# Eight extra two-byte matmuls behind each step's sum, and two-byte chunk tables, in a four-layer graph network

## The reference, cut to what matters

```python
def gcn_conv(x, src, dst, W, b, n_nodes):          # layer 0, twice
    h = x @ W
    msg = h[src] * (dinv[src] * dinv[dst])[:, None]
    return jax.ops.segment_sum(msg, dst, num_segments=n_nodes) + b

for _ in range(3):                                 # layer 1
    p = softmax(einsum('ecd,ecd->ec', z, u[trg]))  # z = xc[src]
    u = _l2norm(segment_sum(z * p[:, :, None], trg) + xc)

msg_sum = segment_sum(feature[src], dst)           # layer 2
h = relu((msg_sum / deg_safe[:, None]) @ W + b)

h = gelu(concatenate([H[src], edge_attr]) @ W1 + b1)   # layer 3
x = layernorm(H + segment_sum(h @ W2 + b2, dst)) * gamma + beta
```

## Time and profile before

| What | Value |
|---|---|
| Median of 3 runs | 6748.66 us (6747.69 to 6758.79) |
| Profiled execution, its span from first to last instruction | 7795.8 us |
| TensorE busy / VectorE / ScalarE / GpSimd in the span | 52% / 42% / 14% / 58% |
| Mean granted TensorE clock | 0.665 |
| CONV1, CONV2, MEAN in the span | 1146, 1138, 1142 us |
| CAPS1, CAPS2, CAPS3, EDGE in the span | 1407, 509, 510, 1347 us |

### The profile page before, as it was taken

How to read it: one execution, slowest core, us unless ns; L and a number is a source line. 1 busy time by engine, 2 the same in 40 slices (tenths; PEclk the granted TensorE clock), 3 DMA queues, 4 the chain that set the end, 5 groups by cost and what they waited for, 6 DMA issues and landing times.

```text
span 7795.8 us, 105357 instructions
## 1 busy us (share of the span) xinstructions
PE 4038.3 (52%) x24944; PEld 3239.4 (42%) x24945; DVE 3241.9 (42%) x8240; ACT 1099.4 (14%) x2520; POOL 4491.4 (58%) x4619
## 2 busy tenths in 40 slices
PE   0333334333333455555558868823333347777776
PEld 0323323333233345544557767713333334444443
DVE  4222213222124555555578888842221243333335
ACT  0000000000001222222233343310000021111112
POOL 4666665666664555555535535546666635555553
PEclk9656656556566676667789989955665565555555
DMA  3111112111111333333347757711111111111111
GB/s 98 44 45 45 45 46 54 44 46 45 45 45 29 118 118 119 118 118 119 120 151 224 225 176 228 223 47 44 45 45 45 45 41 38 38 39 38 39 38 39
DMA packets 354854, 637.41 MB, mean 82 GB/s; under 512 B 85485, under 2 KB 120442, under 8 KB 354170
## 3 DMA queue, kind: packets, MB, share of 16 engines
q0 software_dynamic: 127936, 263.97, 13.5%
q10 hardware_dynamic: 105408, 191.94, 7.9%
q1 hardware_dynamic: 121466, 181.04, 6.8%
HBM read 500.81 MB, written 135.79 MB: 82 GB/s over the span
## 4 chain that ended last, share of the span: by engine, by line
another core or an unknown queue 35%; PE 24%; issue 16%; DVE 12%; DVEq 5%; DMA 4%; ACT 3%; ACTq 1%; SPq 0%; POOL 0%; POOLq 0%
PE ps_sum L606 15%; PE ps_u L661 4%; PE ps_u L639 4%; DMA hots<-hot_rows 3%; DVE zu L1190 2%; DVE onehot L1000 2%; DVEq L241 2%; DVE acc L1014 1%; DVEq L1014 1%; DVE logit L1199 1%; ACT hots L808 1%; PE ps_a L656 1%; DVE prob_n L1174 1%; ACT onehot L818 1%
## 5 line engine op out<-in xcount | busy, mean ns | idle before, releaser
L525 POOL DMA_INDIRECT ring<-table,rows_idx x3920 | 3874.4, 988 | 2436.8 <-issue 1126.9
L606 PE MATMUL ps_sum<-ring,onehot 128*128 x5856 | 1202.3, 380 | 2328.5 <-DVE onehot L1000 1047.7
L606 PEld LDWEIGHTS ps_sum<-ring,onehot 128*128 128x128 f32 x5856 | 1078.6, 280 | 2452.1 <-issue 2450.5
L1014 DVE TENSOR_TENSOR acc<-ps_sum,acc 128x128 f32 x1708 | 492.2, 288 | 3140.0 <-remote 2336.3
L606 PE MATMUL ps_sum<-msg,onehot 128*128 128x128 f32 x7808 | 1479.8, 349 | 33.3 <-POOL msg L311 21.9
L606 PEld LDWEIGHTS ps_sum<-msg,onehot 128*128 128x128 f32 x7808 | 1285.1, 249 | 432.0 <-issue 396.5
L639 PE MATMUL ps_u<-u_parts,hots 128*128 x8784 | 763.8, 239 | 790.1 <-ACT hots L808 364.8
L1000 DVE SCALAR_TENSOR_TENSOR onehot<-dst,minus_row,iota 128x512 f32<-128x512 f32 x1220 | 913.8, 749 | 239.8 <-issue 211.9
L639 PEld LDWEIGHTS ps_u<-u_parts,hots 128*128 128x128 bf16 x8784 | 619.9, 106 | 915.0 <-issue 880.4
L311 POOL TENSOR_TENSOR msg<-ring,prob_n 128x512 f32<-128x512 f32 x488 | 516.9, 1059 | 614.6 <-DVE prob_n L1174 581.8
L1190 DVE TENSOR_TENSOR zu<-ps_u,ring 128x512 f32<-128x512 f32 x732 | 503.1, 687 | 594.8 <-remote 283.8
(11 more groups left out here) (149 smaller groups left out, 1919.9 us busy)
## 6 DMA issues: line engine op xcount, KB each, us to landing
hots<-hot_rows ACTq DMA_DIRECT2D x488, 256.0 KB, 3.5
ring<-z_rows SPq DMA_DIRECT2D x392, 256.0 KB, 3.6
ring<-table,rows_idx POOLq DMA_INDIRECT x3920
hot_rows<-hots ACTq DMA_DIRECT2D x244, 256.0 KB
z_rows<-ring SPq DMA_DIRECT2D x196, 256.0 KB
table<-acc SPq DMA_DIRECT2D x9, 1024.0 KB, 5.1
x<-in_x SPq DMA_DIRECT2D x1, 3328.0 KB, 11.6
table<-h SPq DMA_DIRECT2D x4, 832.0 KB, 4.4
```

The costliest lines, as they stand in the source:

```text
L525: nc.gpsimd.indirect_dma_start(out=ring[:, j, t * P:(t + 1) * P], out_offset=None, in_=tables[p], in_offset=bass.IndirectOffsetOnAxis(ap=r ...
L606: last = nc.tensor.matmul(ps_sum[k % 2][:, 0:P], lhsT=onehot[:, k % HOTS, t, :], rhs=rows(t), start=(t == 0), stop=(t == TILES - 1))
L1014: V.tensor_tensor(acc_flat[:, at], ps_sum[k % 2][:, 0:P], acc_flat[:, at], ALU.add)\
```

## The change

After the four matmuls of a step's sum in the plain passes, eight matmuls follow that multiply the two-byte identity with a two-byte operand of 512 columns (the identity four times), into `ps_b`, a bank of which nothing reads what they write. They wait for nothing and raise nothing. The tables `key_row` and `chunk_tab` become unsigned two-byte integers in place of four-byte ones.

```diff
+IDLE_MATMULS = 8
...
-        key_row = sb("key_row", [1, CHUNKS], i32)
+        key_row = sb("key_row", [1, CHUNKS], u16)
...
-        chunk_tab = sb("chunk_tab", [1, 256], i32)
+        chunk_tab = sb("chunk_tab", [1, 256], u16)
...
+            idle_rows = ident16[:, :].unsqueeze(1).to_broadcast([P, TILES, P])
+
             def plain_pass(p):
                 def body(s, k, chunk, have):
                     pe.wait_ge(landed, chunk(0) + (1 + CHUNKS * p))
                     rows = ring_flat[:, ds(ring_at(chunk(0)), TILES * P)]
                     sum_step(s, k, p, lambda t: rows[:, t * P:(t + 1) * P])
+                    for _ in range(IDLE_MATMULS):
+                        nc.tensor.matmul(ps_b[:, :], lhsT=ident16[:, :], rhs=idle_rows, start=True, stop=True)
                 over_steps(pe, ENGINE.PE, body, 0)
```

More of the change, by code:

```diff
@@ L46, in build @@
           w_edge, b_edge, w_out, b_out, gamma, beta, out):
-    fp32, bf16, i32 = mybir.dt.float32, mybir.dt.bfloat16, mybir.dt.int32
+    fp32, bf16, i32, u16 = mybir.dt.float32, mybir.dt.bfloat16, mybir.dt.int32, mybir.dt.uint16
     ALU = mybir.AluOpType
```

## The result

The changed kernel takes 6949.03 us (median of 4, 6944.7 to 6958.21) against 6749.41 us; the ratio is 1.0297, interval 1.0283 to 1.0312. It is 200 us slower. The forecast was 6750 us with a range to 6840.

The account below looks back on a forecast made before the run. The prediction took GpSimd's 1.25 us per gather, 980 us a pass, to bound the plain passes, with TensorE slack. Matmuls, pass ends and tables at 0 each, carried over to the median 6748.66, gave 6750 us, range 6690 to 6840.

Parts of the forecast that it names:

- the two-byte tables: Register loads from the tables: time goes with bytes, -57 us, or with the number of values, 0; taken as 0.
- faster B: Rival: the table loads halve in time, -57 us, giving 6692 us; chance 0.10.
- The matmuls, taken as 0: Plain passes: eight added matmuls per step cost 0, with ends of -31 us and +937 to +1376 us.
- The mechanism of cover: Plain passes: at full clock, TensorE's 2.8 to 3.4 us per step hide under the gathers' 4.02 us.
- The faster sums: Plain passes: sums end 0.7 to 1.0 us sooner at the full clock, but off the path, so 0.
- The ends of the passes: Last added matmuls before the node product: +1 to +8 us, cancelled by its start at full clock; taken as 0.
- The slow rival on the clock: Plain passes: TensorE, lacking the full clock, becomes the bound; +15 to +60 us, 6964 or 7686 us; chance 0.25.
- The reason given, the recording: Whole program: the span's 1047.1 us above the median were placed in line 417 stalls that an unrecorded execution mostly lacks.
- faster A: Rival: late semaphores exist without recording and a TensorE that never rests ends them; -31 to -86 us, chance 0.15.

Follow-up runs that it names:

- e2: Kernel after without the added matmuls, so the two-byte tables alone: 6951.81 us against 6758.69, ratio 1.0281.
- e3: Kernel before with masked waits, plus a two-byte table of chunk numbers read in CAPS2 and CAPS3 alone: 6926.94 us against 6758.69, ratio 1.0255.
- e8: No added matmuls, only SyncE's table key_row made two bytes wide: 6745.0 us against 6748.92 for the kernel before, ratio 0.9993.
- e1: Kernel after with both tables back at four bytes, so the eight matmuls alone, waits masked with 255: 6783.63 us against 6758.69, ratio 1.0038.
- e5: Four-byte tables and sixteen added matmuls per step in place of the eight of e1: 6939.49 us against 6748.92 for the kernel before, ratio 1.0282.
- e4: Kernel before with only an AND with 255 on the values that waits use: 6754.58 us against 6758.69, ratio 0.9992.
- e6: Kernel before with masked waits, the edge pass's attribute matmul widened from 12 to 128 rows with zeros: 6609.02 us against 6748.92, ratio 0.9794.
- e7: Kernel before with masked waits, plus two two-byte matmuls per step in the edge pass: 6614.75 us against 6748.92, ratio 0.98.
- e9: Kernel of e1 with the eight matmuls ahead of the sum, on another chip: 7894.12 us against 7776.33 for the kernel before, ratio 1.0152.
- e12: Kernel of e1 with four added matmuls per step, on a third chip: 7907.84 us against 7846.59 for the kernel before, ratio 1.0075.
- e11: Kernel of e9 again, on a third chip: 7962.79 us against 7846.59 for the kernel before, ratio 1.0144.

## Why the prediction was wrong

**The step that failed is the two-byte tables, taken as 0.** The prediction priced them by "if the time goes with bytes, -57 us; if it goes with values, 0". Both ends rest on the time of four-byte loads, and there was no row of a two-byte load. It gave no end above nothing, although the operation was one that the trace did not show. Measured: 233 ns per value in place of 64, 193 us by themselves (e2), 168 of them in CAPS2 and CAPS3 (e3). The path was in the prediction, as the 1.7% of the chain that are VectorE's loads, but it was used for the saving alone. Among the rivals there was a mechanism of the tables only on the faster side (faster B), and the slower one was put on the clock.

**The floor of a load.** The Trainium skill ("DMA: Bandwidth & Descriptors", section "Latency and other measured facts") gives a load some 600 ns as a floor. The runs do not bear it out as a floor: 4 four-byte values take 337 ns. The 592 ns of 8 four-byte values lie near it, but 8 two-byte values take 1930 ns. What counts in these runs is the number of values, their width and, for four-byte ones, where the load starts (e8).

**The matmuls, taken as 0, cost 25 us** (0.38%, 0.24 to 0.52%). The two parts do not quite add up: 193 + 25 = 218 us against 200 together. Each of the three has an interval of about 10 us to either side, so whether they add is not shown. The mechanism of cover holds. TensorE's load per step was put at 2.8 to 3.4 us and is 2.6 (e1); the granted clock was taken near 1.0 and is 0.92; GpSimd's pace is the bound, and with sixteen the time is what the working for e5 has. What was missed is small: CONV1, CONV2 and MEAN are 3 to 7 us longer each. GpSimd's gathers over the whole program in e4 and in e1:

```profile
L525 POOL DMA_INDIRECT ring<-table,rows_idx x3920 | 3835.2, 978 | 1557.5 <-issue 1112.8 <-DMA table<-h 143.8 <-DMA table<-acc 143.0
```

```profile
L526 POOL DMA_INDIRECT ring<-table,rows_idx x3920 | 3857.3, 984 | 1552.1 <-issue 1111.1 <-DMA table<-h 142.0 <-SPq L418 140.2
```

The mean rose from 978 to 984 ns, 3920 x 6 ns = 24 us, and in the plain passes nothing hides the gathers. The other kernels agree only roughly: without the matmuls the mean is 974 to 978 ns in e3, e6, e7 and e8 but 981 in e2, and with sixteen it is 990. Why they are longer stays open. In CONV1 those above 1.0 us are 44 of 784 in e4 and 112 in e1. Each of them runs beside VectorE's building of `onehot`; none that runs beside the add alone is long. A sum that ends sooner may thus move VectorE's work onto them, but this is argued and not shown. e9 to e12 were to tell and could not.

**The faster sums, taken as 0: right.** A sum of the plain passes takes 1.05 to 1.15 us in place of 2.07, and the passes did not get shorter. The rule that the prediction took from the Trainium skill ("TensorE: Matmul & The Clock Gate", section "What's actually happening"), that activity releases the clock, agrees with CONV1: the granted clock was 0.57 to 0.69 in kernels without the matmuls (e2, e4) and 0.92 with them. The passes gained nothing from it. In EDGE, where TensorE was busy for 1036 of 1142 us, the clock stayed at 0.50, so being busy was not enough there.

**The ends of the passes, taken as 0: right.** From the last add of CONV1 to the first sum of CONV2 are 43 us in e4 and 41 in e1.

**The slow rival on the clock** did not come about in the plain passes with eight matmuls. Its evidence, the edge pass at 0.50, is real but of another cause: with 128 rows in place of 12 the same number of columns gets 0.84 (e6).

**What bounds the kernel.** That an execution of 6749 us has hardly any stalls of line 417 left was right: e4 has CONV1 at 993 us with a floor of 980. The reason given, the recording, was wrong. Every run of e1 to e12 has a span on record that is 2 or 3 us below its own time, and on two other chips the time of the kernel before is itself 7776 and 7847 us. The rows of before, with their span of 7795.8 us and the same "remote" waits, most likely come from such a chip; their chip is not on record. What differs is not known. Rival faster A, that a busy TensorE ends the late semaphores, found no support on those chips: the matmuls made the kernel slower there by 61 to 118 us, and the late semaphores stayed.

## What to carry to other kernels

An operation whose form the trace does not hold, be it only another width or another start of the same load, has an end of its range on the slower side, and the chain tells where it would be paid: here in the two passes where several engines load at the start of each turn. A pass that leaves TensorE busy at half the clock deserves a look at how many rows of the array its matmuls use; zero rows up to 128 gave 140 us here. Before rows are used as prices, compare span and median; if they differ by more than a per cent or two, the rows may come from a chip on which the bound is another.

## What the runs showed that was not expected

- Loading two-byte values from SBUF into registers takes 233 ns per value against 64 ns for four-byte ones, on TensorE; VectorE and GpSimd have 3.6 us for 16 values as well, against 1.1. The 64 ns were seen only in loads that start at a multiple of four values: SyncE's four-byte loads of 14 values take 1.17 us from such a start and 2.87 us from any other, as long as the two-byte ones.
- In the edge pass, TensorE was busy for 1036 of 1142 us and had a granted clock of 0.50 throughout. With 116 zero rows more in one of its matmuls it had 0.84, with two added two-byte matmuls per step 0.71, and the pass fell from 1142 to 997 and 995 us.
- The kernel before takes 6749 to 6759 us where e1 to e8 ran, and 7776 and 7847 us on two other chips. There the passes without gathers are as fast as on the first (e11: CAPS2 and CAPS3 508 and 509 us), and in those with gathers VectorE waits up to 30 us for semaphores of TensorE's matmuls that rise late.
